# Preparation and attention in one block, with the gate-weight jobs in the attention steps

## The reference, cut to what matters

```python
# heads 16, head size 64, causal mask: k_pos <= q_pos
def xattn(query, key, value):
    q, k, v = split_heads(query @ w_q), split_heads(key @ w_k), split_heads(value @ w_v)
    scores = einsum('bhqd,bhkd->bhqk', q, k) * 64 ** -0.5 + mask
    return merge(einsum('bhqk,bhkd->bhqd', softmax(scores), v)) @ w_o

def ffn(x):                      # qdq: to 16 bits by the largest magnitude of the whole tensor
    x = act_qdq(x)
    up = act_qdq(x @ lpbq(w_up).T)      # lpbq: 4 bits, one scale per 32 inputs
    gate = act_qdq(x @ lpbq(w_gate).T)
    gate = act_qdq(gate * u16(sigmoid(gate)))
    return act_qdq(gate * up) @ lpbq(w_down).T

x = x + tanh(g_xattn) * xattn(layernorm(x), ctx, ctx)
x = x + tanh(g_ffn) * ffn(layernorm(x))
```

## Time and profile before

| | us |
|---|---|
| median of 3 runs (1512.80 to 1517.58) | 1515.35 |
| the profiled execution, its own time | 1512.33 |
| its span, first to last instruction | 1510.5 |
| TensorE busy in it | 1331.8 (88%) |
| VectorE busy | 1097.1 (73%) |
| ScalarE busy | 596.8 (40%) |
| POOL busy | 241.3 (16%) |
| mean granted clock of TensorE, as a share of 2.4 GHz | 0.947 |

### The profile page before, as it was taken

How to read it: one execution, slowest core, us unless ns; L and a number is a source line. 1 busy time by engine, 2 the same in 40 slices (tenths; PEclk the granted TensorE clock), 3 DMA queues, 4 the chain that set the end, 5 groups by cost and what they waited for, 6 DMA issues and landing times. The chain is left out here.

```text
span 1510.5 us, 18719 instructions
## 1 busy us (share of the span) xinstructions
PE 1331.8 (88%) x6141; PEld 1089.7 (72%) x6141; DVE 1097.1 (73%) x1460; ACT 596.8 (40%) x705; POOL 241.3 (16%) x249
## 2 busy tenths in 40 slices
PE   6589999999999985999999989999994009999999
PEld 5468877877886864788888868887883008888887
DVE  5557878878878853667777769998998995455453
ACT  2232232232223212334443335556667973333331
POOL 2112211212212210000100025551101000000000
PEclk9889999999999986999999989999997559999999
DMA  8701211211110117866665689996558863444443
GB/s 290 253 0 36 70 40 53 68 42 49 62 56 35 50 46 300 295 230 236 230 245 191 221 317 309 312 317 214 173 191 322 336 239 120 172 148 167 162 151 118
DMA packets 110998, 259.17 MB, mean 172 GB/s; under 512 B 10848, under 2 KB 23136, under 8 KB 109408
## 3 DMA queue, kind: packets, MB, share of 16 engines
q1 hardware_dynamic: 110656, 258.52, 49.0%
q10 hardware_dynamic: 288, 0.00, 0.0%
HBM read 151.52 MB, written 106.95 MB: 171 GB/s over the span
## 5 line engine op out<-in xcount | busy, mean ns | idle before, releaser
L1065 PE MATMUL gpG<-xph,Wh 128*128 128x512 f32 x384 | 153.1, 399 | 2.0 <-DVE xpl L985 2.0
L1539 PE MATMUL pD<-Wh,xph 128*128 128x512 f32 x384 | 150.3, 391 | 4.6 <-DVE xpl L1518 4.6
L1065 PE MATMUL pU<-xph,Wh 128*128 128x512 f32 x384 | 150.8, 393 | 0.7 <-POOLq L63 0.7
L1065 PE MATMUL gpG<-xph,Wl 128*128 128x512 f32 x384 | 150.7, 393 | 0.0
L1065 PE MATMUL gpG<-xpl,Wh 128*128 128x512 f32 x384 | 150.6, 392 | 0.0
L1065 PE MATMUL pU<-xpl,Wh 128*128 128x512 f32 x384 | 150.5, 392 | 0.0
L1065 PE MATMUL pU<-xph,Wl 128*128 128x512 f32 x384 | 150.3, 392 | 0.0
L1539 PE MATMUL pD<-Wl,xph 128*128 128x512 f32 x384 | 150.1, 391 | 0.0
L1539 PE MATMUL pD<-Wh,xpl 128*128 128x512 f32 x384 | 150.1, 391 | 0.0
L1518 DVE TENSOR_TENSOR xpl<-doq,xph 128x1536 fp32r<-128x1536 int16 (+1 forms) x34 | 56.4, 1664 | 122.8 <-ACT xph L1485 122.8
L968 ACT ACTIVATE gst<-gpG,sc 128x512 f32<-128x512 f32 x96 | 66.4, 692 | 170.3 <-PE gpG L1065 164.5
(11 more groups left out here) (169 smaller groups left out, 2912.6 us busy)
## 6 DMA issues: line engine op xcount, KB each, us to landing
dub<-up_d SPq DMA_DIRECT2D x42, 768.0 KB, 4.7
gate_d<-gst SPq DMA_DIRECT2D x96, 256.0 KB, 2.5
gb<-gate_d SPq DMA_DIRECT2D x32, 768.0 KB, 6.3
up_d<-ust SPq DMA_DIRECT2D x96, 256.0 KB, 4.4
xr<-xn_d SPq DMA_DIRECT2D x9, 1024.0 KB, 6.1
xph<-up_d SPq DMA_DIRECT2D x11, 768.0 KB, 6.0
xpl<-up_d SPq DMA_DIRECT2D x11, 768.0 KB, 6.1
xin<-in_x SPq DMA_DIRECT2D x32, 256.0 KB, 2.7
```

The costliest lines, as they stand in the source:

```text
L1065: mm = pe.matmul(ps[:, :], Ws[:, it, kt * P:(kt + 1) * P], xs[:, kt, :], start=(kt == 0 and Ws is Wh and xs is xh), stop=(kt == KT - 1 and ...
L1539: mm = pe.matmul(pD[4 * t + q][:, :], os_[n][:, cs], Ws[:, it, :], start=(it == 0 and os_ is oh and Ws is Wh), stop=(it == IT - 1 and os_ ...
```

## The change

One function, `front_phase`, takes the place of `prepare` and `attend`: one block, no barrier between them. The score banks pS serve as PSUM for the preparation, and Ah, Al, Vh, Vl take the place of w_q, w_k and w_v in SBUF. TensorE does the k projections with w_q's turns between them, then the v projections, and goes straight on to the attention steps. The twelve gate-weight jobs leave the preparation; four of them lie in each of the three passes of the loop, with two buffers and with pX as their PSUM bank. x's turn in step 8 (and 0) moves behind the values. The second normalisation moves from VectorE to ScalarE, for which POOL makes a third small value (-mean/deviation); POOL now does the deviation of tile k-3 first. The largest magnitude is spread through TensorE and not by POOL. The number of job buffers becomes a property of each set of jobs; the gate phase keeps its three. SP's loads come in the order context, w_k's first half, w_q's first half, w_k's second, w_q's second, x tiles 0 and 1, w_v, x tile 2, w_o, x tiles 3 to 7, two jobs. The core of the diff, in the order SP, POOL, ScalarE, VectorE, TensorE:

```diff
+        JB = 4
+        J = Jobs(mk, ph, "pj", JB, 2, [pX])
+        with ExitStack() as early:
+            wk = sb(early, "wk", [P, KT, INNER], F32)
+            wv = sb(early, "wv", [P, KT, INNER], F32)
+            wq = sb(early, "wq", [P, KT, INNER], F32)
...
+        Ah = sb(ph, "Ah", [P, KT, INNER], F32R)
+        pw = [pS[0][:, 0:512], pS[0][:, 512:1024]]
+        pk, pv = pS[1][:, 0:512], pS[1][:, 512:1024]
...
+        def job_at(k, jobs, delay):
+            q = k - 3 - delay
+            return q if jobs and 0 <= q < JB else None
...
         @block.sync
...
+                q = job_at(k, jobs, 2)
+                if q is not None:
+                    job_store(sp, J, b, q, job_dst(b, q))
+                q = job_at(k, jobs, 1)
+                if q is not None:
+                    job_load(sp, J, b, q + J.NJ, job_src(b, q + J.NJ))
...
+            def rstd2(b, j):
...
+                pool.tensor_scalar(rs2[:, n, 2:3], mv2[:, n, 0:1], rs2[:, n, 1:2], -1.0, ALU.mult, ALU.mult).then_inc(rstd2_done, 1)
             def step(b, k, have, jobs):
+                if have(k - 3):
+                    rstd2(b, k - 3)
                 if have(k + 2):
+                    rstd(b, k + 2)
                 if have(k - 1):
...
+                q = job_at(k, jobs, 0)
+                if q is not None:
+                    job_divide(pool, J, b, q)
-            pool.partition_all_reduce(T1, T0, P, RMAX).then_inc(sx_all, 1)
...
                         act.activation(pTh[:, cs], pT[:, cs], ACT.Copy).then_inc(pTh_done, 1)
+                q = job_at(k, jobs, 2)
+                if q is not None:
+                    job_hi(act, J, b, q)
...
+                def normal2():
+                    if have(k - 3):
...
+                        act.activation(x2[j % 2][:, :], x1[j % 2][:, :], ACT.Identity, bias=rs2[:, j % 2, 2:3],
+                                       scale=rs2[:, j % 2, 1:2]).then_inc(x2_done, 1)
                 if which == 0:
                     high()
+                normal2()
...
                         dve.tensor_tensor(pTl[:, cs], pT[:, cs], pTh[:, cs].bitcast(F32), ALU.subtract).then_inc(pTl_done, 1)
+                q = job_at(k, jobs, 2)
+                if q is not None:
+                    job_lo(dve, J, b, q)
                 early = which is not None or not have(BQ)
                 if early and have(k - 3):
                     residual(b, k - 3)
                 if have(k - 1):
                     scores_down(b, k - 1)
                 if not early and have(k - 3):
                     residual(b, k - 3)
+                q = job_at(k, jobs, 1)
+                if q is not None:
+                    job_integer(dve, J, b, q)
                 if which == 0:
                     some(2)
-                if have(k + 2):
+                if have(k + 2) and k + 2 >= 2:
                     statistics(b, k + 2)
                 some(2 if which == 0 else 1)
+                q = job_at(k, jobs, 0)
+                if q is not None:
+                    job_scale(dve, J, b, q)
                 if have(k - 1):
                     sums(b, k - 1)
                 some(2 if which == 0 else 1)
-                if have(k + 2):
+                if have(k + 2) and k + 2 >= 2:
                     normal(b, k + 2)
-                some(1)
-                if have(k - 3):
-                    normal2(b, k - 3)
-                some(1)
+                some(2)
                 if which == 0:
                     some(8)
                 if have(k + 1):
...
+                some(2)
+                if have(k - 3):
+                    largest(b, k - 3)
                 some(8)
...
+                if which != 0:
+                    if have(k) and k >= 0:
+                        scores(b, k)
+                    turn_x()
                 values(b, k, have)
                 if which == 0:
+                    turn_x()
                     scores(b, k)
+                q = job_at(k, jobs, 1)
+                if q is not None:
+                    pe.wait_ge(*tile(xl_done, b, k + 1))
+                    job_turn(pe, J, b, q, ident)
...
+            for r in range(ROUNDS):
+                project(wk, r, wk_in, [(k_sb, r - 1)] if r >= 2 else [], k_ps)
...
+            for r in range(ROUNDS):
+                project(wv, r, wv_in, [(k_sb, 3 + r)] if r < 2 else [(v_sb, r - 1)], v_ps)
             schedule(pe, step)
+            pe.wait_ge(sx_red, 1)
+            everywhere(pe, pX[:, 0:P], T0, ident).then_inc(sx_spread, 1)
```

More of the change, by code:

```diff
@@ L128, in flamingo_block @@
          T0, T1, T2, T3, T4, AMAX, GPOS, GNEG, AP2, AN2) = [sc[:, n:n + 1] for n in range(25)]
[L130 to L143, removed]
+        front_phase(mk, xf, cf, (w_q, w_k, w_v, w_o), g_xattn, g_ffn, w_src[0], wsc[0], x1_d, xn_d, ident, mask, half, xmx,
+                    (TG_X, TG_F, RAW_X, RAW_F, S_X, INV_X, T0, T1))
+        release_sems()
         with ExitStack() as ff:
@@ L189, in __init__ @@
         self.inv = sb(ph, f"{tag}inv", [P, NJ, NBLK], F32)
-        self.bank = [pb(ph, f"{tag}bank{n}") for n in range(banks)]
+        self.bank = bank
         self.loaded = [sem(f"{tag}_loaded{n}") for n in range(NJ)]
@@ L279, in by_input, with diagonal @@
     return [d[:, bass.ds(r * (3 * 512) + c * 512, 512)] for d in w]
[L282 to L291, removed]
+def diagonal(act, t, bd, b, done):
+    for a in range(2):
+        rows = slice(a * 64, a * 64 + 64)
+        act.activation(bd[rows, :, a * 64:a * 64 + 64], t[rows, :, bass.ds(CK * b, CK)], ACT.Copy).then_inc(done, 1)
@@ L471, in attend @@
+        vT = sb(ph, "vT", [P, PAIRS, B * CK], F32)
+        kbd = sb(ph, "kbd", [P, PAIRS, P], F32)
+        vbd = sb(ph, "vbd", [P, PAIRS, P], F32)
+        xin = [sb(ph, f"xin{n}", [P, H], F32) for n in range(BQ)]
         xn = [sb(ph, f"xn{n}", [P, H], F32) for n in range(2)]
@@ L568, in step @@
-            def step(b, k, have):
+            pool.memset(ident[:, :], 0.0).then_inc(const_set, 1)
+            pool.memset(mask[:, :], 0.0).then_inc(const_set, 1)
+            pool.memset(half[:, 0:1], -0.5).then_inc(const_set, 1)
+            pool.memset(half[:, 1:2], LN_EPS).then_inc(const_set, 1)
+            pool.wait_ge(const_set, 4)
+            pool.affine_select(out=ident[:, :], in_=ident[:, :], compare_op=ALU.not_equal, fill=1.0,
+                               base=0, pattern=[[-1, P]], channel_multiplier=1).then_inc(id_set, 1)
@@ new lines, in _, with rstd @@
+            pool.affine_select(out=mask[:, :], in_=mask[:, :], compare_op=ALU.is_ge, fill=-10000.0,
+                               base=0, pattern=[[-1, CK]], channel_multiplier=1).then_inc(id_set, 1)
+            head_starts(pool, sems)
+            pool.memset(kbd[:, :, :], 0.0).then_inc(bd_zero, 1)
+            pool.memset(vbd[:, :, :], 0.0).then_inc(bd_zero, 1)
+            def rstd(b, j):
+                n = j % 2
+                pool.wait_ge(*tile(mean_done, b, j))
+                pool.wait_ge(*tile(xn_done, b, j - 2))
+                pool.tensor_tensor(rs[:, n, 0:1], mv[:, n, 1:2], half[:, 1:2], ALU.add).then_inc(eps_done, 1)
+                pool.wait_ge(*tile(eps_done, b, j))
+                pool.tensor_tensor(rs[:, n, 1:2], rs[:, n, 0:1], half[:, 0:1], ALU.pow).then_inc(rstd_done, 1)
@@ L766, in chunk @@
                     if n == 0:
[L767 removed]
+                        pe.wait_ge(kbd_set, 2 * b + 2 * ahead + 2)
                     for q in range(4):
@@ L812, in scores, with step @@
                 mm.then_inc(s_ps, 1)
-            def step(b, k, have):
+            def step(b, k, have, jobs):
                 which, ahead = matrices(k, have)
```

372 lines of the change are left out of this document (158 added, 214 removed).

## The result

| us | before | changed |
|---|---|---|
| median, lowest to highest of 5 runs each | 1515.82 (1512.80 to 1517.58) | 1504.05 (1501.93 to 1508.61) |
| the profiled execution, its own time (span) | 1512.33 (1510.5) | 1506.39 (1504.6) |
| first scores | 90.59 | 54.04 |
| gate phase's first load | 574.87 | 566.10 |
| TensorE, VectorE, ScalarE, POOL busy | 1331.8, 1097.1, 596.8, 241.3 | 1333.7, 1041.1, 620.1, 253.2 |

The ratio is 0.9929 [0.9907, 0.9951]: 0.7% faster, a small gain that can be measured, where I forecast none. The two profiled executions differ by 5.9 us only, the medians by 11.8; that difference is part of the story.

A forecast was written before the change was run, and what follows sets the result against it. TensorE bounds attention, with little VectorE room; preparation waits on DMA, jobs and barriers. -32.9 - 3.2 + 16.2 + 3.6 + 4.5 + 13.8 = +2.0 us on 1512.33; median 1515.35 moves to 1517, no measurable change; range 1500 to 1526.

The forecast's parts named there:

- start: Preparation, up to the first score matmul: first scores at 57.7 us instead of 90.59, gain 32.9 us, bounds 31 to 35.
- job steps: Attention steps k=3 to 7: jobs' VectorE work lengthens the chain to POOL's probabilities, loss 5.4 us a block, 16.2 in all.
- step 8: Attention step 8: last job's low part ahead of the residual, x's turn behind the values; loss 1.2 us a block.
- steps 9 and 10: VectorE's maximum of x2 ahead of two low chunks, behind ScalarE's x2: scores start 1.5 us later, 4.5 for three blocks.
- clock falls: Behind the new gaps of 3.1 and 2.9 us TensorE's clock falls: 2.3 us each, 13.8 in all, bounds 0 and 17.4.
- drain: End of the attention phase, in steps without scores: no change of its own in the forecast sum.
- end: Last maximum to the gate phase's first load: spread through TensorE instead of POOL, gain 3.2 us, bounds 1 to 4.
- The weighed cost: job_integer's product beside POOL's second deviation: taken as 0.69 us, unblocked; by the skill's rule up to 8 us worse.
- The clock stays up: Rival: no falls behind the new gaps, 13.8 us go, 1503; one place falling, 1510. Chance 0.30, one or both places.
- VectorE is held up by POOL: Rival: job_integer in k=4 to 7 takes up to 0.66 us longer each, 7.9 in all, 1525; chance 0.20.
- The start is bound by loads: Rival: wk and wq come as late as in the old order; each 5 us costs 5, 1522; chance 0.08.
- The jobs find room: Rival: VectorE runs the jobs' work in its waits, half of the 16.2 us goes, 1509; chance 0.06.

## Why the prediction was wrong

Against the first profile, up to the gate phase's first load:

| term | forecast | measured |
|---|---|---|
| start | -32.9 | -36.6 |
| job steps | +16.2 | +15.3 |
| step 8 | +3.6 | +3.2 |
| steps 9 and 10 | +4.5 | +5.0 |
| clock falls | +13.8 | +7.3 |
| drain | 0 | -0.4 |
| end | -3.2 | -2.7 |
| sum | +2.0 | -8.9 |

The last column is worked out from the timelines: first scores 54.04 - 90.59; for steps the differences to the table above, three times, with steps 8 and 10 of the passes without a fall (22.81 and 12.49); the end from the rows 563.22 and 566.10 (-3.45) and a last tile that is 0.74 longer. The load itself comes 574.87 - 566.10 = 8.8 earlier. The mechanisms and their signs held, except one premise on the clock; two sizes did not.

**The start** (bounds 31 to 35) was 36.6. The failed step is the sum of durations "9.8 + 5.28 + 1.04 + 3 x (3.62 + 1.04) + 4 x 3.62 + 12 handoffs of 0.1": the end of a group overlaps the next one's start, so the terms are 3.46 and 0.87, and no handoff is to be added. With these, the v projections give way to x's turn at 42.5 (measured 42.54) and not at 45.8. Pitches between two starts would have given it; for the chunks I used one, and it held (2.58).

**The clock** has two faults. The step "so I charge 2.3 each, 13.8 in all" mis-sized the fall: mostly 1.5 us, and not behind every gap (1.3 to 2.7 measured, behind four or five of six). And its premise, "The 1.87 gaps (one a block) cost nothing", was one lucky execution: the kernel before has the same falls, 1.5 us each, in the two other executions that were profiled. That its median holds them too is inferred from these two, for its other runs have no profile. So I counted as new a cost that was in part there already, 3 to 4.5 us of it, and then added "3.0 above this execution" to the sum as if it were independent of it. The size makes 6.5 us and the 3.0 added on top make 3.0 of the 13.3 by which 1517.35 was too high, and the start makes 3.7. The other terms, off by 0.7 together, and the scatter of the executions nearly cancel.

The profiles differ by 5.9 and the medians by 11.8 because the profile of before was a short execution, 3.5 under its median, and that of the changed kernel a long one, 2.3 over its own. From the gate phase's first load to the end of the span the three profiles of before take 935.6, 935.8 and 934.7 us, the changed kernel's two 938.5 and 935.3: its first profile lost 3 us there. Over all fourteen profiles this part, whose code is the same, takes 933.9 to 940.7. Which gap is followed by a fall and which not stays open.

**The job steps** were right to 0.2 us a step, and the run without jobs bears the total out. What I did not see is what keeps that price low: "it does not shorten the chain" about the second normalisation is true, but it had kept VectorE for 1.99 us, until after POOL's probabilities were done at 187.05, and no row of it stands in the forecast:

```profile
185.33 1.99 DVE L699 TENSOR_SCALAR x<-x,mv,rs 128x512 f32<-128x512 f32 x1
```

With it in its old place the change is worth nothing (1.0002).

**The weighed cost** went as taken, 0.69, but the reason given is only half of it. Timeline of the changed kernel, the product and the small POOL instruction beside it:

```profile
109.49 0.69 DVE L226 TENSOR_TENSOR pjd<-pjq,pjs 128x512 f32<-128x512 int16 x1
109.58 1.01 POOL L479 TENSOR_TENSOR rs<-rs,half 128x1 f32<-128x1 f32 x1
```

The product began first and kept its time; POOL's power, 0.55 alone, took 1.01. The Trainium skill ("SBUF — State Buffer", the section Who interferes with whom) says that a VectorE instruction with two SBUF inputs contends with a GpSimd instruction that reads SBUF, and, of VectorE's two-port mode, that whoever issues first gets the shared ports for its whole instruction and the other fully blocks. These rows of the trace agree, in both directions: here POOL lost and ended 0.41 us after the product, and beside the probabilities, which had begun first, VectorE's conversion (0.39 to 1.53) and x2 (0.49 to 2.13) lost. So a tiny POOL instruction is not outside of this, as I had argued: it is held up itself. But the order of the starts does not settle every pair. In the earlier trace rows POOL's power began 0.18 us ahead of xn and was still the one that got longer (0.67 for 0.55), while xn kept its 0.46; and in neither place does a tiny POOL instruction hold VectorE up. Why stays open.

**The rivals.** "The clock stays up" was the nearest in number: its case with one place falling gives 1510, and the start's 3.7 brings that to 1506. It is not what happened, for the clock fell at both places, in some passes and more cheaply. "VectorE is held up by POOL" is refuted for the changed kernel (all twelve products take 0.692 to 0.694 us). "The start is bound by loads" is refuted: behind the first weight TensorE waits for no load up to the first scores. "The jobs find room" is refuted too: steps 5 and 6 take 14.01 and 13.95, not 12.9.

## What to carry to other kernels

Add up stretches of an engine's work by the distance from start to start; in these rows the durations of matmul groups overlap by 0.16 to 0.17 us. Before a stall is priced by what the clock did behind it, read more than one execution, since the same gap of 1.9 us was followed by a fall in some and not in others, and a cost that the kernel before has already must not be charged to the change. And when work is put into an engine's list, ask for each of its instructions which engine waits for what stands behind it: moving three short pieces gave 21.6 us here, more than the whole change.

## What was not expected of the hardware

A gap of 1.87 us on TensorE was followed by some microseconds at 1.2 GHz in 5 of 9 cases (three profiles of the kernel before); gaps of 2.8 to 2.9 us were followed by it in 9 of 12 in the two profiles of the changed kernel, and in 33 of 42 with those of its variants. With six idle matmuls in a gap of 2.31 the clock stayed at 1.00 in three of three. Step 8 of the third pass kept its clock in both profiles of the changed kernel behind 2.90.

ScalarE's x2, whose scale and bias are columns in memory, takes 0.80 to 0.82 us where a plain copy of the same size takes 0.60; I had taken 0.7. The Trainium skill ("ScalarE: Activation LUTs", the section What ACT_TABLE_LOAD costs) says that each such operand adds about 93 ns. The trace agrees: the estimate from that figure is 0.60 + 2 x 0.093 = 0.79.
